# Norms from sums of squares, the two partial sums of relations added on GpSimd, and one product with the key table

## What is computed

```python
seg = dst * NUM_REL + edge_type                      # 10 relations
xs = x[src]
sums = jax.ops.segment_sum(xs, seg, num_segments=N * NUM_REL)
cnt = jax.ops.segment_sum(jnp.ones(seg.shape, x.dtype), seg, num_segments=N * NUM_REL)
mean = (sums / jnp.maximum(cnt, 1.0)[:, None]).reshape(N, NUM_REL, -1)
return jnp.einsum('nrd,rdo->no', mean, w_rel) + x @ root + bias
# twice: h = relu(layer(x, w_rel1, root1, b1)); y = layer(h, w_rel2, root2, b2)
# then x = layernorm(x + y): (x - mean) / sqrt(var + 1e-5) over the 128 features
```

## Time and profile before

| | us |
|---|---|
| median of three runs | 2550.78 |
| lowest, highest | 2544.63, 2570.12 |
| the profiled execution | 2542.57 |
| its span, first to last instruction | 2540.7 |
| of it the output stage | 1146 to 1344 |
| of it the first relation stage | 1832 to 2173 |
| of it the last stage | 2173.7 to 2540.7 |

### The profile page before, as it was taken

The page is one execution under the profiler, slowest core; times in us unless marked ns, Lnnn a source line. Parts: engine busy times, 40 slices in busy tenths (PEclk is TensorE's granted clock), DMA queues, the critical chain, the costliest instruction groups (busy, mean ns, idle before and its releaser), DMA issues. The chain is left out here.

```text
span 2540.7 us, 52681 instructions
## 1 busy us (share of the span) xinstructions
PE 2126.1 (84%) x12829; PEld 1645.4 (65%) x12829; DVE 2052.9 (81%) x6720; ACT 1474.0 (58%) x4845; POOL 1517.9 (60%) x1653
## 2 busy tenths in 40 slices
PE   2998888889678769997778995677599999899996
PEld 2887777777566559976657883565466666455553
DVE  3566999999679958977996986687588888688886
ACT  0677666667589956764456883677444444233332
POOL 1677888888445456648877883434344443355554
PEclk9999999999899979998998997899799999899998
DMA  5666676676555455556775553344423322212121
GB/s 90 215 226 220 228 224 228 231 230 221 159 162 177 157 152 172 172 155 189 218 211 157 188 188 94 120 152 154 132 65 83 83 81 73 65 54 57 55 58 30
DMA packets 291555, 376.29 MB, mean 148 GB/s; under 512 B 59002, under 2 KB 142896, under 8 KB 291258
## 3 DMA queue, kind: packets, MB, share of 16 engines
q1 hardware_dynamic: 265658, 321.84, 40.0%
q0 software_dynamic: 25600, 51.09, 7.7%
HBM read 167.38 MB, written 206.80 MB: 147 GB/s over the span
## 5 line engine op out<-in xcount | busy, mean ns | idle before, releaser
L1819 PE MATMUL phase_p_w<-phase_w_rel,phase_rowsT 128*128 128x512 f32 (+1 forms) x1200 | 511.4, 528 | 10.0 <-ACT phase_rowsT L1872 9.9
L1900 DVE SCALAR_TENSOR_TENSOR phase_added<-phase_p_w,relation,phase_added 128x128 f32<-128x128 f32 x1200 | 350.0, 340 | 23.0 <-PE phase_p_w L1819 21.1
L779 POOL DMA_INDIRECT phase_rows<-X,src_row x200 | 191.4, 957 | 193.3 <-PE phase_p_T L1827 168.1
L779 POOL DMA_INDIRECT phase_rows<-H,src_row x200 | 192.7, 964 | 135.2 <-PE phase_p_T L1827 109.0
L389 PE MATMUL phase_p_h<-W2c,phase_g 128*128 128x128 f32 x1568 | 204.8, 286 | 57.9 <-ACT phase_g L342 42.7
L389 PEld LDWEIGHTS phase_p_h<-W2c,phase_g 128*128 128x128 f32 x1568 | 194.3, 200 | 82.5 <-issue 80.1
L1819 PEld LDWEIGHTS phase_p_w<-phase_w_rel,phase_rowsT 128*128 128x128 f32 x1200 | 189.6, 193 | 86.6 <-issue 41.4
L543 POOL TENSOR_TENSOR phase_o<-phase_y,phase_r 128x512 f32<-128x512 f32 x98 | 106.7, 1089 | 200.5 <-DVE phase_r L353 199.6
L327 ACT ACTIVATE phase_sq<-phase_y 128x512 f32<-128x512 f32 x294 | 181.5, 632 | 66.1 <-DVE phase_y L456 59.5
L396 PE MATMUL phase_p_g<-phase_x1T,W 128*128 128x512 f32 x392 | 202.6, 598 | 2.6 <-PEq L58 1.7
L348 DVE TENSOR_REDUCE phase_ss<-phase_sq 128x4 f32<-128x512 f32 x294 | 197.9, 673 | 3.4 <-PEq L58 2.5
(11 more groups left out here) (259 smaller groups left out, 6775.7 us busy)
## 6 DMA issues: line engine op xcount, KB each, us to landing
H<-phase_h SPq DMA_DIRECT2D x196, 256.0 KB, 4.2
X<-phase_x SPq DMA_DIRECT2D x196, 256.0 KB, 3.6
phase_same<-same_keys SPq DMA_DIRECT2D x175, 256.0 KB
phase_xT<-in_x_columns SPq DMA_DIRECT2D x98, 256.0 KB, 3.3
Z<-phase_x SPq DMA_DIRECT2D x98, 256.0 KB, 2.3
phase_x<-X SPq DMA_DIRECT2D x98, 256.0 KB
out<-phase_o SPq DMA_DIRECT2D x98, 256.0 KB
H<-R SPq DMA_DIRECT2D x50, 256.0 KB, 2.4
```

The costliest lines, as they stand in the source:

```text
L779: pool.indirect_dma_start(out=out[t % GATHERS][:, :], out_offset=None, in_=table, in_offset=bass.IndirectOffsetOnAxis(ap=index, axis=0)).t ...
L1819: nc.tensor.matmul(p_w[(PARTS * (t % UNROLL) + n) % BANKS][:, 0:b - a, :], rowsT[v][:, :], w[:, a:b, :], start=True, stop=True).then_inc(s ...
L1900: nc.vector.scalar_tensor_tensor(out=added[v][r % 2][:, :], in0=p_w[(PARTS * (t % UNROLL) + n) % BANKS][:, r % RG, :], scalar=plane(D["rel ...
```

## The change

Four edits:

1. In the output stage and the last stage a new class `CentredNorm` takes the place of `Norm`: ACT squares four tiles at once, DVE sums the squares, ACT takes the root of the sum / 128 + eps, DVE the reciprocal. In the output stage DVE multiplies four tiles' rows in one instruction; in the last stage ACT scales each tile's rows in place, and POOL scatters them from `Y`.
2. Without a mean in the norm, the weights must be centred: those of the last stage are loaded in the first relation stage and centred at its end by three DVE instructions. The last stage loads no weights.
3. In both relation stages POOL adds the two partial sums of a tile (`joined`), and PE multiplies `same` once. The add is due in step t + 2, and the product and all that follows one step later than before.
4. The lags behind it grow: the scatter in the last stage is due in step t + 13, the loops run 14 and 16 steps past the last tile instead of 13.

The diff, cut (the last lags of the hidden products and copies, which grow by one each, are left out):

```diff
@@ class CentredNorm, new @@
+    def square(self, act, Y, j):
+        act.wait_ge(self.s["y_full"], UNROLL * (j + 1))
+        wait(act, self.s["squares_added"], j - 1)
+        act.activation(self.squares[j % 2][:, :, :], Y[:, UNROLL * j:UNROLL * (j + 1), :], ACT.Square).then_inc(self.s["squares_full"], 1)
+    def add(self, dve, j):
...
+        self.nc.vector.tensor_reduce(self.total[j % 2][:, :], self.squares[j % 2][:, :, :], AX.X, ALU.add).then_inc(self.s["squares_added"], 1)
+    def deviation(self, act, j):
...
+        act.activation(self.dev[j % 2][:, :], self.total[j % 2][:, :], ACT.Sqrt, bias=self.W["eps"][:, :], scale=1.0 / F).then_inc(self.s["dev_full"], 1)
+    def invert(self, dve, j, rows_before):
...
+        self.nc.vector.reciprocal(self.inverse[j % 2][:, :], self.dev[j % 2][:, :]).then_inc(self.s["inverse_dev_full"], 1)
+def last_of(k, lag):
+    t = at(k, lag)
+    return t // UNROLL if t is not None and t % UNROLL == UNROLL - 1 else None
@@ output_rows, vector @@
-                    if (t := at(k, 13)) is not None:
-                        y = plane(D["Y"], t, 0, F)
-                        norm.rows_of(dve, y, y, t)
...
+                    if (j := last_of(k, 11)) is not None:
+                        norm.invert(dve, j, j - 1)
+                        dve.wait_ge(s["inverse_dev_full"], j + 1)
+                        y = D["Y"][:, UNROLL * j:UNROLL * (j + 1), :]
+                        nc.vector.tensor_tensor(y, y, over_rows(norm.inverse[j % 2]), ALU.mult).then_inc(s["normal_full"], 1)
@@ relation_rows, sync @@
-                sp.dma_start(w[:, :, :], w_rel.rearrange("r p f -> p r f")).then_inc(s["w_loaded"], 16)
+                if hidden:
+                    sp.dma_start(w[:, :, :], io["L3_gnn_w_rel1"].rearrange("r p f -> p r f")).then_inc(s["w_loaded"], 16)
+                    sp.dma_start(D["w_rel2c"][:, :, :], io["L3_gnn_w_rel2"].rearrange("r p f -> p r f")).then_inc(s["w_rel2_loaded"], 16)
@@ relation_rows, gpsimd @@
                     if (t := at(k + 3, 0)) is not None:
                         gather_tile(pool, table, column(D["src_row"], t), rows_, gathered, s["transposed"], t)
+                    if (t := at(k, 2)) is not None:
+                        v = t % 2
+                        pool.wait_ge(s["added_full"], PAIR * (t + 1))
+                        wait(pool, s["summed"], t - 1)
+                        pool.tensor_tensor(joined[v][:, :], added[v][0][:, :], added[v][1][:, :], ALU.add).then_inc(s["joined_full"], 1)
...
-                        if (t := at(k, 11)) is not None:
+                        if (t := at(k, 13)) is not None:
...
-                                                    in_=out_rows[t % GATHERS][:, :], in_offset=None, bounds_check=N - 1,
+                                                    in_=plane(D["Y"], t, 0, F), in_offset=None, bounds_check=N - 1,
@@ relation_rows, tensor @@
-                    if (t := at(k, 2)) is not None:
+                    if (t := at(k, 3)) is not None:
                         v = t % 2
-                        pe.wait_ge(s["added_full"], PAIR * (t + 1))
+                        pe.wait_ge(s["joined_full"], t + 1)
...
-                        nc.tensor.matmul(p_sum[:, 0:F], loads.same(t), added[v][0][:, :], start=True, stop=False)
-                        last = nc.tensor.matmul(p_sum[:, 0:F], loads.same(t), added[v][1][:, :], start=False, stop=t == 0)
+                        last = nc.tensor.matmul(p_sum[:, 0:F], loads.same(t), joined[v][:, :], start=True, stop=t == 0)
@@ relation_rows, scalar @@
+                    if not hidden and (j := last_of(k, 5)) is not None:
+                        norm.square(act, D["Y"], j)
+                    if not hidden and (t := at(k, 12)) is not None:
+                        j, y = t // UNROLL, plane(D["Y"], t, 0, F)
+                        act.wait_ge(s["inverse_dev_full"], j + 1)
+                        act.activation(y, y, ACT.Copy, scale=column(norm.inverse[j % 2], t % UNROLL)).then_inc(s["normal_full"], 1)
@@ relation_rows, vector @@
-                            wait(dve, s["summed"], t - 1)
+                            wait(dve, s["joined_full"], t - 1)
...
+                if hidden:
+                    w2 = D["w_rel2c"]
+                    dve.wait_ge(s["w_rel2_loaded"], 16)
+                    nc.vector.tensor_reduce(mean[:, :], w2[:, :, :], AX.X, ALU.add).then_inc(s["w_rel2_step"], 1)
...
+                    nc.vector.tensor_scalar(mean[:, :], mean[:, :], -1.0 / F, None, ALU.mult).then_inc(s["w_rel2_step"], 1)
...
+                    nc.vector.tensor_tensor(w2[:, :, :], w2[:, :, :], mean[:, :].unsqueeze(2).to_broadcast([F, RELATIONS, F]),
+                                            ALU.add).then_inc(s["w_rel2_step"], 1)
```

More of the change, by code:

```diff
@@ L1730, in _, with relation_rows @@
                 beside.dense.all_stored(sp)
-def relation_rows(nc, io, W, D, table, w_rel, hidden):
+def relation_rows(nc, io, W, D, table, w, hidden):
     RG, PAIR = 4, RELATIONS - 2
@@ L1739, in relation_rows @@
     BANKS = 4 if hidden else 2 * PARTS
-    STEPS = T + 13
+    STEPS = T + 14 if hidden else T + 16
     with Phase(nc) as m:
@@ L1840, in _ @@
                     multiply(k, 2)
-                    if hidden and (t := at(k, 6)) is not None:
+                    if hidden and (t := at(k, 7)) is not None:
                         v = t % 2
@@ L1845, in _ @@
                         nc.tensor.matmul(p_out[:, 0:F], hT[v][:, :], W["root2c"][:, :], start=True, stop=True).then_inc(s["out_multiplied"], 1)
-                    if hidden and (t := at(k, 5)) is not None:
+                    if hidden and (t := at(k, 6)) is not None:
                         pe.wait_ge(s["h_full"], t + 1)
@@ L1853, in _ @@
                 for k in range(STEPS):
-                    if hidden and (t := at(k, 4)) is not None:
+                    if hidden and (t := at(k, 5)) is not None:
                         v = t % 2
@@ L1904, in _ @@
                 for k in range(STEPS):
-                    if hidden and (t := at(k, 7)) is not None:
+                    if hidden and (t := at(k, 8)) is not None:
                         dve.wait_ge(s["out_multiplied"], t + 1)
@@ L1966, in gnn_kernel @@
             gat_rows(nc, io, W, D, beside)
-        relation_rows(nc, io, W, D, io["X3"], io["L3_gnn_w_rel1"], hidden=True)
-        relation_rows(nc, io, W, D, io["H"], io["L3_gnn_w_rel2"], hidden=False)
+        weights = Memory(nc, stack)
+        w_rel1, D["w_rel2c"] = weights.sb("w_rel1", [F, RELATIONS, F]), weights.sb("w_rel2c", [F, RELATIONS, F])
+        relation_rows(nc, io, W, D, io["X3"], w_rel1, hidden=True)
+        relation_rows(nc, io, W, D, io["H"], D["w_rel2c"], hidden=False)
 _INS = ['x', 'edge_attr_42', 'L0_gnn_Wq', 'L0_gnn_bq', 'L0_gnn_Wk', 'L0_gnn_bk', 'L0_gnn_Wv', 'L0_gnn_bv', 'L0_gnn_Ws', 'L0_gnn_bs',
```

85 lines of the change are left out of this document (46 added, 39 removed).

## The result

The changed kernel takes 2480.97 us (median of four runs, 2478.74 to 2485.92), the kernel before 2547.7 in the same session: a ratio of 0.9714, with a 95% interval from 0.9653 to 0.9776. The forecast was 2490, with a range from 2467 to 2518. The profiled executions are 2542.57 and 2478.74 us long, so the step to be explained is -63.8 us; the forecast's sum was -60.

The account below looks back on a forecast made before the run. PE was taken to bound the first relation stage, PE-DVE hand-overs with DVE's long list the last, POOL the output stage. -40.7 - 17.2 - 2 = -60 from 2542.6 gave 2483, on the median's scale 2490, range 2467 to 2518.

Parts of the forecast that it names:

- PE in the first relation stage: First relation stage: PE alone sets 3.27 us per tile; one product less gives 3.05, -20.9 us over about 95 tiles.
- The centring: End of the first relation stage: DVE centres the second set of weights with other engines idle, +3.3 us.
- What held the last stage before: Last stage before the change: PE and DVE hand tiles to each other, DVE with the long list, 3.39 us per tile.
- POOL as the new bound of the last stage: Last stage: POOL's gather, add, scatter and gaps sum to 2.93 us per tile, above PE's 2.72; taken as 2.95.
- The bound's worth: Last stage: 82 tiles at 2.95 us where each took 3.39, with a longer scatter tail, -40.7 us in all.
- DVE's list: Last stage: DVE's work falls to 2.53 us per tile and a small reciprocal, under POOL's 2.93.
- the second rival: Relation stages: DVE and POOL shut each other out of shared ports; last stage 3.1 us per tile, kernel 2508; chance 0.17.
- The output stage: Output stage: norms from squares free DVE, which POOL doesn't wait for except in the tail; taken as -2 us.
- nothing on one side: Output stage: the new norm's least gain is nothing, its greatest some 5 us of the tail.
- The loads: Weight loads move from the last stage's start to the first relation stage's start; taken as 0, with 2 us either side.
- The late gathers: Last stage: each gather stands behind an earlier tile's add and comes too late; kernel some 2620 us; chance 0.04.
- The total: Whole kernel: -60 us, so 2483 against the profiled execution; 2490 on the scale of the median, 8 us above it.

## Why the prediction was right, step by step

**PE in the first relation stage: right.** 95 x 0.22 = -20.9 was forecast for PE; from the first transposition to the last it is -23.8 (321.4 to 297.6), 2.2 in every ten steady tiles and 3.6 in the first ten, which the forecast had left out in part. At the start 0.7 us come on top (7.4 us to the first transposition instead of 6.7, the loads beside it), and the end is 3.1 us longer (13.4 to 16.5). No run puts the second product back in this stage; its 0.22 us is read from the timeline here, and measured in the last stage, where PE's list with and without it is 2.93 and 2.71.

**The centring: the size right, the reason half of it.** Its +3.3 is the stage's longer end (+3.1). One of its parts is right by luck: two and a half times 0.67 is 1.68 us and not the 1.5 written; the row took 1.47. And it had a twin that the forecast didn't see: the add keeps POOL at work until the last tile, and POOL's drain ends 8.25 us after its last instruction. In the changed kernel the two end within 0.3 us of each other (9.29 us from POOL's last add to the next clear against the 8.97 above, where only the drain is left), so that taking away the centring gained nothing and taking away both gained 3.4 us; the add on POOL alone wasn't taken away in this stage.

**What held the last stage before: half right.** The forecast named the hand-overs between PE and DVE and DVE's long list. PE did wait for the eighth add, but once in four tiles it waited behind ACT, whose root waited 2.0 us for DVE's moments (36.1 us over 18 times). The forecast had no term for that wait; it went with the new norm, whose root is due a step after the sum that it reads, and whether that step or the shorter list took it away stays open.

**POOL as the new bound of the last stage: right.** 2.94 against the sum of 2.93, gap for gap. The first 13 tiles took 2.67 instead of 2.8, since without a scatter PE's list alone counts. The 12 scatters span 14.2 us as forecast.

**The bound's worth: right in sum, wrong in what it implied.** The forecast let the product's 0.22 us and POOL's add be the story of both relation stages. In the last stage the add on POOL bought only its step of slack, and put POOL's 2.94 where PE alone would have given 2.71. The forecast's own list had that: PE 2.72, POOL without the add 2.6, DVE 2.53 with room for one more add. It didn't ask which of the three should do the add.

**DVE's list: too long.** The sums from SBUF were taken with their length of 0.28 us; they occupy 0.20 from start to start.

**The ports (the second rival): the reason against them was wrong, the verdict right.** The forecast said that POOL's add follows the eighth add at once. It does in the first relation stage. In the last stage POOL comes to it later, in its own time: the add of 2256.80 runs while DVE already does the last four adds of the next tile (from PSUM), which it doesn't hold (0.34 us each beside it as without it). They still miss each other, in 78 of 82 tiles, and where they were made to meet, DVE's room took it. The rival's 3.1 us per tile was mis-sized, since it charged DVE's loss in full to a stage that POOL sets, and the loss itself was 0.09 us per tile (280 to 367 ns), not 0.46. Nor does the row of 1.84 us bear out all of the cited rule: by the profile that DVE instruction had started 0.39 us ahead of the addition, and it was the one held. The row shows that the two shut each other out, not that the first to start holds the ports.

**The output stage: wrong in sign.** -2 was forecast and +1.0 came, +2.3 in the mean of the twelve kernels with the new norm (200.3 against 198.0). The step that failed is "nothing on one side": the bound reckoned only with a shorter list on DVE, not with the new instruction's 0.69 us on two operands in SBUF beside a POOL that is the bound. The Trainium skill (SBUF — State Buffer, section "SBUF: two separate sides") states that while DVE runs an instruction in its two-port mode, GpSimd is locked out of the shared ports and can't write the descriptors of its DMAs. For the descriptors it names that mode alone, and not an instruction with two operands in SBUF. The gather of 1.46 us instead of 0.96 would fit the same lock with such an instruction on DVE; no run here shows that the descriptors are what waits. The forecast used the section only for the add.

**The loads: right.** +0.7 us at the first relation stage's start, -1.1 at the last stage's (5.6 us to the first transposition instead of 6.7).

**The late gathers (a rival): they didn't come.** In the steady last stage POOL's gathers follow its scatters with no more than their own gap. The rival's price was also a little off: 4.1 instead of 2.95 us per tile for 100 tiles makes some 2605, not 2620.

**The total: right, with some luck.** The two relation stages gave 5.5 us more than forecast, the output stage 3.0 less, and untouched stages gave another 1.4. The rest of the 9 us between 2490 and 2481 lies in the scale: the forecast put the median 8 us above the profiled execution, and after the change it was 2.2 above it.

## What to carry to other kernels

When work moves off the bounding engine, write the per-tile sums of all engines after the move, and give the work to the one where the largest sum stays smallest; here that was DVE (2.71), not POOL (2.94). A result that is used one step later can be worth more than the work that was saved to get it, and costs only a third buffer. A wait in one engine's list holds up all that stands behind it, also what a third engine needs: ACT's root ahead of ACT's copy. An engine that is given work up to a stage's end brings its own end-of-stage time with it, and that hid here what the centring cost, so that taking the centring away alone gained nothing.

## What the runs showed of the hardware that was not expected

Where a block of the program issued gathers, POOL's queue closed it with a drain that ended 8.25 us after POOL's last instruction (7.93 in the block with two gathers per tile), in every trace here; in blocks without DMAs of POOL it ended 0.07 us after it. At the end of the last stage the drain took 7.9 to 8.0 us behind the last scatter's landing. In the output stage it stands in the 8.9 us before the next clear:

```profile
L1039 POOL MEMSET phase_link<- 128x512 f32 x3 | 1.5, 524 | 8.9 <-POOLq L58 8.9
```

What the drain waits for the profile doesn't show, and it wasn't tried apart. Beside a DVE instruction of 128x512 with two operands in SBUF some gathers that POOL issued took 1.2 to 1.46 us instead of 0.96. And on DVE and POOL the start of the next addition of 128x128 comes ahead of the end that the row shows, 0.20 us after a start for 0.28 on DVE and 0.41 for 0.46 on POOL, so that lengths overstate a list of small instructions.
